# Attention pass of a decoder layer: ScalarE's squares, the energy product and the scale put in another place

## The chip, the cores and the metric

The kernel runs on one core of one Trainium2 chip. The metric is the device time of one execution in microseconds (us); several runs are taken and the median is given.

## What is computed

The layer has a self-attention that reduces to a layer norm of x (a general path for inputs that need it is behind a branch and is not taken here), a cross attention against a context, and a feed-forward part. The change touches the cross attention, for 16 batches of 256 rows by 2048 columns:

```
sim = einsum('ncs,nds->ncd', key, query) * C ** (-0.5)
sim = softmax(sim, axis=1)
context = einsum('ncd,nds->ncs', sim, value)
x = layernorm(x + context)
```

Key and value are both the context input, the query is the normalised x. Products are made of float16 pairs (a high and a low part), so the context is first brought to a power-of-two scale that comes from its sum of squares.

## The kernel before

`attention_pass` (tag "fast") runs the 16 batches as a software pipeline, written out by hand on each engine. `batch_slots` calls `slot(n, ...)` for n = -2 to 15. In slot n each engine works on up to three batches: the end of batch n (its context products, additions and second norm), the middle of batch n + 1 (transposing its normalised x into q, logits, softmax, a guard transform) and the beginning of batch n + 2 (statistics and first norm of x, sum of squares, scale, high and low parts of the values). Tiles that two batches need are doubled and chosen by parity. Each engine runs its instructions in the order written; a wait on a semaphore holds up everything behind it on that engine.

TensorE's slot (`slot` under `block.tensor`): three transposed banks of q (L612), the guard's inverse products (L638), then eight context groups of six products (L625), each of the first five followed by another transposed bank; then the logits of batch n + 1 in two groups of 48 products (L649, `logits(0)` and `logits(1)`), and the guard's forward transform (L689). A transposed bank p waits until bank p - 3 is free, that is until VectorE has made its q_lo. The energy product (L600, `context_energy`) adds the sums of squares of batch n + 2 over the partitions; it stands between the seventh and the eighth context group, and in slot -1 behind the first logits group. `logits(1)` waits for `scale_ready`, because the energy's result lies in its bank.

ScalarE's slot: eight q_hi copies of transposed banks (L347, `emptied_bank`), and between them the deviation squares of the second norm (L391, `spread2`), its application (L397, `normalise2`) and four half-tile squares of the context (L355, `square_context`, 128 x 1024 with an accumulated sum). Then `normalise2` of the first half, the high parts of the values (L422, `value_high`, which waits for the scale), the first norm (L377), exponentials (L384), squares of a weight tile (L370, in slot -1 and odd slots) and of the guard (L428). The squares of the context wait for the context's load, first half in `cbuf0`, second half in `cbuf1`; each also waits for the square before it.

VectorE's slot: eight times q_lo of a bank (L470, `emptied_bank`) and a context addition (L495), with the guard's maxima (L476) between; then `context_scale` (L484, L100 to L102, L486), the mean (L459, L461), statistics of x for batch n + 2 (L552, `x_stats(0)`), low parts of the values (L529), softmax maxima (L536), folds (L565), `x_stats(1)`, probabilities (L543 to L545).

SyncE issues every load and store on one queue, in order: the stores of batch n - 1 (L245, the second waits for `normalise2`), the weight tile in slot -1 and odd slots (L239), the two halves of x for batch n + 2 (L252, each waits until the context additions of batch n are done with its half), the transposes of the keys (L229) and the context for batch n + 3 (L221).

Of the kernel before, what the change touches and what calls it, by code (L numbers as in the profile page):

```python
# [39 lines left out]
KT = L // P  # L40
# [50 lines left out]
def is_batch(n, nb):  # L91

    return not isinstance(n, int) or 0 <= n < nb
# [18 lines left out]
def attention_pass(nc, src, ctx_in, x2_out, w_chunks, b_rows, ag_in, consts, stored, eps_column, tag):  # L112
# [3 lines left out]
    nb = src.shape[0] // C  # L116
    w_rows = w_chunks.rearrange("c p o -> (c p) o")
    PIECES = 2 * R
    with ExitStack() as st:
# [92 lines left out]
        CG = R * NBANK  # L212

        with nc.Block() as block:
# [121 lines left out]
            def _(act):  # L336
                def slot(n, half, parity):
                    cur, nxt, n2 = is_batch(n, nb), is_batch(n + 1, nb), is_batch(n + 2, nb)
# [10 lines left out]
                    def square_context(i):  # L349

                        if n2:
                            r, at = i // 2, i % 2 * HALF
                            act.wait_ge(c_loaded[r], 16 * (n + 3))
                            after(act, sumsq_done, PIECES * (n + 2) + i)
                            nc.scalar.activation(junk[:], cbuf[r][:, at:at + HALF], ACT.Square,  # L355
                                                 accum_out=sumsq[parity][:, i:i + 1]).then_inc(sumsq_done, 1)
# [43 lines left out]
                    for j in range(CG):  # L400
                        emptied_bank(j)
                        if j == 1 and is_batch(n - 1, nb):
                            spread2(n - 1, other, 1)
                        if j == 3 and is_batch(n - 1, nb):
                            normalise2(n - 1, other, 1)
                        if j == 5 and cur:
                            spread2(n, parity, 0)
                        if 1 <= j <= PIECES and n != -1:
                            square_context(j - 1)
                    if n == -1:  # L410
                        for i in range(PIECES):
                            square_context(i)
                    if cur and n < nb - 1:
                        normalise2(n, parity, 0)
                    if n == nb - 1:
# [30 lines left out]
            def _(dve):  # L446
# [5 lines left out]
                def slot(n, half, parity):  # L452
                    cur, nxt, n2 = is_batch(n, nb), is_batch(n + 1, nb), is_batch(n + 2, nb)
# [34 lines left out]
                    for j in range(CG):  # L488
# [22 lines left out]
                        if j == 4 and n == nb - 1:  # L511
                            chain.link(v.tensor_reduce(tmp2[:, 0:1], g_lags[:], AX.X, ALU.max))
                            v.tensor_scalar(verdict[:, 1:2], tmp2[:, 0:1], -GUARD_GAP, None, ALU.is_gt).then_inc(w_summed, 1)
                    if n != -1:
                        context_scale()
                    if cur:

# [47 lines left out]
                            v.tensor_tensor(u_t[:, :, at], q_hi[:, 0:k, at], q_hi[:, k:KT, at], ALU.subtract).then_inc(folded, 1)  # L565

                    x_stats(0)
                    if n == -1:
                        context_scale()
                    value_low(0)  # L570
                    softmax_max(0)
# [16 lines left out]
            def _(pe):  # L588
                def slot(n, half, parity):
# [52 lines left out]
                    def logits(r):  # L642

                        after(pe, exp_done, R * n + r + 1)
                        terms = [(q_hi, 0), (q_hi, 1), (q_lo, 0)]
                        for i in range(3 * KT):
                            qq, part = terms[i % 3]
                            k = i // 3
                            ins = nc.tensor.matmul(ps_s[r][:, 0:C], qq[:, k, r * P:(r + 1) * P], k_both[other][:, k, part, :],  # L649
                                                   start=(i == 0), stop=(i == 3 * KT - 1))  # L650
                        ins.then_inc(sim_done, 1)
# [7 lines left out]
                    for j in range(CG):  # L659
                        if cur:  # L660
                            context(j)
                        if j + 3 < TQ:
                            transposed_bank(j + 3)
                        if j == 6 and n == nb - 1:
                            pe.wait_ge(w_summed, 4)
                            nc.tensor.matmul(verdict_all, ones[:], verdict[:], start=True, stop=True).then_inc(w_reduced, 1)
                        if j == 6 and n != -1:
                            context_energy()
                    if nxt:

                        pe.wait_ge(k_turned, 16 * 2 * R * (n + 2))
                        pe.wait_ge(t_free, TQ * (n + 1) + TQ // R)
                        after(pe, g_free[1], n + 1)
                        logits(0)
                        if n == -1:
                            context_energy()

                        pe.wait_ge(t_free, TQ * (n + 2))
                        if n2:
                            pe.wait_ge(scale_ready, n + 3)  # L680
                        logits(1)

                        pe.wait_ge(folded, R * (n + 2))
                        if isinstance(n, int) and n == -1:
                            pe.wait_ge(tables_loaded, 32)
                        after(pe, ctx_added, CG * (n + 1))
                        for m in range(4):
                            for k in range(HALF // P):
                                ins = nc.tensor.matmul(ps_f[m][:, 0:C], fwd[:, k, m * P:(m + 1) * P], u_t[:, k, :],  # L689
                                                       start=(k == 0), stop=(k == HALF // P - 1))  # L690
                            ins.then_inc(fwd_done, 1)
# [1266 lines left out]
```

## Time and profile before

| | us |
|---|---|
| median of 3 runs | 1969.69 |
| lowest and highest run | 1968.1, 1973.83 |
| profiled execution, its time | 1971.83 |
| its span in the profile | 1970.0 |
| TensorE busy | 1785.7 (91%) |
| VectorE busy | 1363.3 (69%) |
| ScalarE busy | 794.9 (40%) |
| GpSimd busy | 201.2 (10%) |

The span is what the profile's time stamps cover. Shares of busy time are over the whole span; the attention pass is roughly its first 570 us, the feed-forward part the rest, and the two have different limits, so the pass has to be read by itself. In the rows below PE is TensorE, PEld its weight loads, DVE VectorE, ACT ScalarE, POOL GpSimd, SPq SyncE's queue of DMA issues.

### The profile page before, as it was taken

To read this page: it belongs to the slowest core of one execution; us is meant where nothing else is said; L and a number is where in the kernel's file an instruction comes from. 1 tells how busy PE (TensorE), PEld (TensorE's weight loads), DVE (VectorE), ACT (ScalarE), POOL (GpSimd) and SP (SyncE) were. 2 spreads that over 40 slices of the span, in tenths; PEclk is the share of its full clock that TensorE was granted. 3 is DMA by queue.
4 is the path that set the end of the run, shared out by engine and by line. 5 is a ranking of instruction groups with operands and counts; after the bars stand their busy time and mean duration, and the time that the engine had idled before them with its cause. 6 is when DMAs were issued, how large, how long until landed. Compare 5 with 4: busy or idle time off the path is not lost. (4 is left out here: it accounts for less than half of the span.)

```text
span 1970.0 us, 27015 instructions
## 1 busy us (share of the span) xinstructions
PE 1785.7 (91%) x10194; PEld 957.3 (49%) x10210; DVE 1363.3 (69%) x2605; ACT 794.9 (40%) x939; POOL 201.2 (10%) x358
## 2 busy tenths in 40 slices
PE   3989999999853959999999999997899999999997
PEld 2666665757531425444554445443344444444443
DVE  3878887878759856677766677789655555465463
ACT  5788888788745221222222222233221222213111
POOL 1223232323200000000000000000010010010000
PEclk9999999999985989999999999999899999999999
DMA  8899999999848499999999999955999889988982
GB/s 278 194 279 272 283 251 282 267 282 244 234 181 239 121 237 252 264 255 238 252 249 252 251 240 224 232 171 160 275 262 257 274 222 261 265 247 244 255 243 107
DMA packets 565563, 472.70 MB, mean 240 GB/s; under 512 B 498416, under 2 KB 502512, under 8 KB 544624
## 3 DMA queue, kind: packets, MB, share of 16 engines
q1 hardware_dynamic: 565424, 470.87, 87.6%
q8 instruction: 84, 1.38, 0.3%
q14 instruction: 55, 0.45, 0.1%
HBM read 237.51 MB, written 109.58 MB: 176 GB/s over the span
## 5 line engine op out<-in xcount | busy, mean ns | idle before, releaser
L1558 PE MATMUL bank_f<-w_hi_f,a_cols_f 128*128 128x512 f16 x3584 | 1093.4, 382 | 76.9 <-DMA a_cols_f<-rows_f 61.4
L1558 PE MATMUL bank_f<-w_lo_f,a_cols_f 128*128 128x512 f16 x1792 | 685.0, 382 | 0.0
L1558 PEld LDWEIGHTS bank_f<-w_hi_f,a_cols_f 128*128 128x128 f16 x3584 | 352.8, 98 | 508.0 <-issue 45.4
L1148 ACT ACTIVATE rows_f<-xn_f 128x1024 f16<-128x1024 f32 x78 | 82.4, 1056 | 499.5 <-DMA xn_f<-x_scratch 339.8
L1558 PEld LDWEIGHTS bank_f<-w_lo_f,a_cols_f 128*128 128x128 f16 x1792 | 176.4, 98 | 205.0 <-issue 4.8
L1323 DVE SCALAR_TENSOR_TENSOR y_f<-bank_f,w_iscale_f,y_f 128x512 f32<-128x512 f32 x192 | 134.6, 743 | 169.2 <-PE bank_f L1558 168.9
L649 PE MATMUL ps_s_fast<-k_both_fast,q_hi_fast 128*128 128x256 f16 x1024 | 171.0, 275 | 7.4 <-DMA k_both_fast<-v_lo_fast 6.4
L1284 DVE TENSOR_TENSOR rows_f<-xn_f,rows_f 128x1024 f16<-128x1024 f32 x78 | 94.5, 1211 | 97.3 <-ACT rows_f L1148 97.3
L1323 DVE SCALAR_TENSOR_TENSOR y_f<-bank_f,w_iscale,y_f 128x512 f32<-128x512 f32 x192 | 134.9, 745 | 38.2 <-PE bank_f L1558 32.9
L1284 DVE TENSOR_TENSOR rows_f<-sums_f,rows_f 128x1024 f16<-128x1024 f32 x63 | 76.9, 1221 | 114.5 <-ACT rows_f L1148 114.2
L1148 ACT ACTIVATE rows_f<-sums_f 128x1024 f16<-128x1024 f32 x63 | 66.3, 1053 | 198.8 <-DMA a_cols_f<-rows_f 196.3
L649 PE MATMUL ps_s_fast<-k_both_fast,q_lo_fast 128*128 128x256 f16 x512 | 140.6, 275 | 0.0
L495 DVE SCALAR_TENSOR_TENSOR x2buf_fast<-ps_c_fast,iscale_fast,xbuf_fast 128x512 f32<-128x512 f32 x128 | 95.6, 747 | 42.6 <-PE ps_c_fast L625 42.4
L612 PE MATMUL ps_t_fast<-ident,xbuf_fast 128*128 128x128 f32 x512 | 78.0, 288 | 49.4 <-DVE q_lo_fast L470 36.3
L470 DVE TENSOR_TENSOR q_lo_fast<-ps_t_fast,q_hi_fast 128x512 f16<-128x512 f32 x128 | 87.8, 688 | 40.7 <-ACT q_hi_fast L347 40.6
L649 PEld LDWEIGHTS ps_s_fast<-k_both_fast,q_hi_fast 128*128 128x128 f16 x1024 | 100.9, 99 | 23.3 <-DMA k_both_fast<-v_lo_fast 6.8
L625 PE MATMUL ps_c_fast<-v_hi_fast,p_hi_fast 128*128 128x512 f16 x256 | 99.0, 387 | 0.3 <-DVE x2buf_fast L495 0.3
L625 PE MATMUL ps_c_fast<-v_lo_fast,p_hi_fast 128*128 128x512 f16 x256 | 99.0, 387 | 0.0
L625 PE MATMUL ps_c_fast<-v_hi_fast,p_lo_fast 128*128 128x512 f16 x256 | 98.7, 385 | 0.0
L1200 ACT ACTIVATE cbuf<-cbuf,nb_f,rs_f 128x1024 f32<-128x1024 f32 x16 | 19.8, 1239 | 195.2 <-POOL nb_f L1128 195.2
L612 PEld LDWEIGHTS ps_t_fast<-ident,xbuf_fast 128*128 128x128 f32 x512 | 60.0, 146 | 77.6 <-DVE q_lo_fast L470 57.1
L377 ACT ACTIVATE xbuf_fast<-xbuf_fast,nb_fast,rs_fast 128x2048 f32<-128x2048 f32 x32 | 67.1, 2097 | 41.2 <-POOL nb_fast L299 41.2
(210 smaller groups left out, 2310.8 us busy)
## 6 DMA issues: line engine op xcount, KB each, us to landing
xbuf_fast<-x SPq DMA_DIRECT2D x32, 1024.0 KB, 7.3
x_scratch<-x2buf_fast SPq DMA_DIRECT2D x32, 1024.0 KB, 6.4
y_f<-x_scratch SPq DMA_DIRECT2D x32, 1024.0 KB, 7.9
xn_f<-x_scratch SPq DMA_DIRECT2D x62, 512.0 KB, 4.8
kept_scratch<-a_cols_f SPq DMA_DIRECT2D x45, 512.0 KB, 3.4
xn<-x_scratch SPq DMA_DIRECT2D x45, 512.0 KB, 6.9
a_cols_f<-kept_scratch SPq DMA_DIRECT2D x45, 512.0 KB, 8.9
cbuf<-ctx_in SPq DMA_DIRECT2D x16, 1024.0 KB, 5.9
```

The lines of the kernel that those rows point to most:

```text
L377: nc.scalar.activation(xbuf[parity][:, r], xbuf[parity][:, r], ACT.Identity, bias=nb1[:, r:r + 1], scale=rs1[:, r:r + 1]).then_inc(x1_read ...
L470: v.tensor_tensor(q_lo[at], bank, q_hi[at], ALU.subtract).then_inc(t_free, 1)
L495: v.scalar_tensor_tensor(x2buf[parity][:, r, b * BANK:(b + 1) * BANK], ps_c[j % 2][:], iscale[parity][:], xbuf[parity][:, r, b * BANK:(b + ...
L612: ins = nc.tensor.transpose(bank[:, i * P:(i + 1) * P], xbuf[other][:, r, (kk + i) * P:(kk + i + 1) * P], ident[:])
L625: ins = nc.tensor.matmul(ps_c[j % 2][:], pp[:, d, r * P:(r + 1) * P], vv[parity][:, d, b * BANK:(b + 1) * BANK], start=(i == 0), stop=(i = ...
L649: ins = nc.tensor.matmul(ps_s[r][:, 0:C], qq[:, k, r * P:(r + 1) * P], k_both[other][:, k, part, :], start=(i == 0), stop=(i == 3 * KT - 1))
L1148: nc.scalar.activation(rows[g % 2][:, 0], source(i), ACT.Copy).then_inc(a_hi, 1)
L1200: nc.scalar.activation(data[:, 0], data[:, 0], ACT.Identity, bias=nb_[:, 0:1], scale=rs[:, 0:1])
L1284: v.tensor_tensor(rows[g % 2][:, 1], source(i), rows[g % 2][:, 0], ALU.subtract).then_inc(a_lo, 1)
L1323: v.scalar_tensor_tensor(acc, bank[bank_of(s, origin)][:], (w_iscale if sign > 0 else minus_iscale)[s // NP_][:], acc, ALU.mult, ALU.add). ...
L1558: ins = nc.tensor.matmul(bank[i][:], a_cols[:, i, part + kk, :], ww[:, W_SLOT[i], kk, :], start=(kk == 0 and part == 0 and ww is w_hi), st ...
```

## The change

Four things move, all in `attention_pass`. On ScalarE the four context squares go behind the eighth q bank in every slot (as they were in slot -1), the application of the second norm to the second half goes from behind the fourth bank to behind the fifth, and the deviation square of the first half from behind the sixth bank to behind the seventh. On TensorE the energy product goes from between the context groups into the first logits group, ahead of its product 32 of 48. On VectorE `context_scale` goes from ahead of the mean and the first statistics of x to behind them (as it was in slot -1). Slot -2 runs as before, and slots 14 and 15 have no squares, energy or scale. No instruction is added or removed, and no DMA is moved in the queue.

```diff
@@ ScalarE @@
                         emptied_bank(j)
                         if j == 1 and is_batch(n - 1, nb):
                             spread2(n - 1, other, 1)
-                        if j == 3 and is_batch(n - 1, nb):
+                        if j == 4 and is_batch(n - 1, nb):
                             normalise2(n - 1, other, 1)
-                        if j == 5 and cur:
+                        if j == CG - 2 and cur:
                             spread2(n, parity, 0)
-                        if 1 <= j <= PIECES and n != -1:
-                            square_context(j - 1)
-                    if n == -1:
-                        for i in range(PIECES):
-                            square_context(i)
+                    for i in range(PIECES):
+                        square_context(i)
                     if cur and n < nb - 1:
                         normalise2(n, parity, 0)
@@ VectorE @@
-                    if n != -1:
+                    if n == -2:
                         context_scale()
                     if cur:
...
                     x_stats(0)
-                    if n == -1:
+                    if n != -2:
                         context_scale()
                     value_low(0)
@@ TensorE @@
                         for i in range(3 * KT):
+                            if r == 0 and i == 2 * KT:
+                                context_energy()
                             qq, part = terms[i % 3]
...
-                        if j == 6 and n != -1:
-                            context_energy()
+                    if n == -2:
+                        context_energy()
                     if nxt:
...
                         logits(0)
-                        if n == -1:
-                            context_energy()
```

The diff is three lines shorter, so lines behind L413 carry a number lower by three in the changed kernel.

ScalarE before, in slot 1, from the first context square to the last two q banks (junk with sumsq is a context square, junk2 a deviation square, q_hi a bank):

```order
L355 ACTIVATE junk_fast,sumsq1_fast<-cbuf0 128x1024
L347 ACTIVATE q_hi_fast<-ps_t2_fast 128x4x128
L355 ACTIVATE junk_fast,sumsq1_fast<-cbuf0 128x1024
L347 ACTIVATE q_hi_fast<-ps_t0_fast 128x4x128
L397 ACTIVATE x2buf0_fast<-x2buf0_fast,nb2_fast,rs2_fast 128x2048
L355 ACTIVATE junk_fast,sumsq1_fast<-cbuf1_fast 128x1024
L347 ACTIVATE q_hi_fast<-ps_t1_fast 128x4x128
L355 ACTIVATE junk_fast,sumsq1_fast<-cbuf1_fast 128x1024
L347 ACTIVATE q_hi_fast<-ps_t2_fast 128x4x128
L391 ACTIVATE junk2_fast,ssq21_fast<-x2buf1_fast,nmean21_fast 128x2048
L347 ACTIVATE q_hi_fast<-ps_t0_fast 128x4x128
L347 ACTIVATE q_hi_fast<-ps_t1_fast 128x4x128
```

The same slot in the changed kernel, from the third q bank to the first high part of the values:

```order
L347 ACTIVATE q_hi_fast<-ps_t2_fast 128x4x128
L347 ACTIVATE q_hi_fast<-ps_t0_fast 128x4x128
L347 ACTIVATE q_hi_fast<-ps_t1_fast 128x4x128
L397 ACTIVATE x2buf0_fast<-x2buf0_fast,nb2_fast,rs2_fast 128x2048
L347 ACTIVATE q_hi_fast<-ps_t2_fast 128x4x128
L347 ACTIVATE q_hi_fast<-ps_t0_fast 128x4x128
L391 ACTIVATE junk2_fast,ssq21_fast<-x2buf1_fast,nmean21_fast 128x2048
L347 ACTIVATE q_hi_fast<-ps_t1_fast 128x4x128
L355 ACTIVATE junk_fast,sumsq1_fast<-cbuf0 128x1024 x2
L355 ACTIVATE junk_fast,sumsq1_fast<-cbuf1_fast 128x1024 x2
L397 ACTIVATE x2buf1_fast<-x2buf1_fast,nb2_fast,rs2_fast 128x2048
L419 ACTIVATE v_hi1_fast<-cbuf0,scale1_fast 128x2048
```

The four squares have left the banks and stand between the last bank and the norm of the first half (x2buf1), ahead of the high parts.

VectorE before, in slot 1, from the last context addition to the first statistics (L484 to L486 is the scale, BN_STATS the statistics of x):

```order
L495 SCALAR_TENSOR_TENSOR x2buf_fast,x2sum_fast<-ps_c_fast,iscale_fast,xbuf_fast 128x512
L484 TENSOR_REDUCE tmp_fast<-ps_s_fast 128x1
L100 TENSOR_SCALAR tmp_fast<-tmp_fast 128x1
L101 TENSOR_SCALAR scale_fast<-tmp_fast 128x1
L102 TENSOR_SCALAR iscale_fast<-tmp_fast 128x1
L486 TENSOR_SCALAR lscale_fast<-iscale_fast 128x1
L459 TENSOR_REDUCE tmp_fast<-x2sum_fast 128x1
L461 TENSOR_SCALAR nmean_fast<-tmp_fast 128x1
L552 BN_STATS stats_fast<-xbuf_fast 128x6 x4
```

And in the changed kernel:

```order
L492 SCALAR_TENSOR_TENSOR x2buf_fast,x2sum_fast<-ps_c_fast,iscale_fast,xbuf_fast 128x512
L456 TENSOR_REDUCE tmp_fast<-x2sum_fast 128x1
L458 TENSOR_SCALAR nmean_fast<-tmp_fast 128x1
L549 BN_STATS stats_fast<-xbuf_fast 128x6 x4
L74 MEMSET pad 128x1
L554 BN_AGGR mv_fast<-stats_fast 128x2
L481 TENSOR_REDUCE tmp_fast<-ps_s_fast 128x1
L100 TENSOR_SCALAR tmp_fast<-tmp_fast 128x1
L101 TENSOR_SCALAR scale_fast<-tmp_fast 128x1
```

The scale's chain stands behind the mean, the statistics and their aggregate, and so behind the load of x.

## Rows read from the trace of the kernel before

**Rows 1.** Busy time by stretches, all engines: stretch, length, PE, PEld, DVE, ACT, POOL, PEclk, DMA share.

```profile
63.40:527.70 464.30, 428.38 (x3039) 303.84 (x3053) 382.76 (x882) 383.74 (x502) 127.98 (x248) 0.99 0.94 264
```

**Rows 2.** Timeline of TensorE, slots 8 and 9: start, duration, instruction, idle before and releaser.

```profile
343.61 0.38 PE L649 MATMUL ps_s_fast<-k_both_fast,q_hi_fast 128*128 128x256 f16 x2
...
343.94 0.38 PE L649 MATMUL ps_s_fast<-k_both_fast,q_hi_fast 128*128 128x256 f16 x2
...
360.62 0.38 PE L625 MATMUL ps_c_fast<-v_hi_fast,p_hi_fast 128*128 128x512 f16 x1
...
366.13 0.66 PE L612 MATMUL ps_t_fast<-ident,xbuf_fast 128*128 128x128 f32 x4 [0.57 <-DVE q_lo_fast L470]
...
372.00 0.66 PE L612 MATMUL ps_t_fast<-ident,xbuf_fast 128*128 128x128 f32 x4 [2.19 <-DVE q_lo_fast L470]
...
376.51 0.38 PE L649 MATMUL ps_s_fast<-k_both_fast,q_hi_fast 128*128 128x256 f16 x2
```

**Rows 3.** Busy time in the stretch from T of slot 8 to C of slot 9.

```profile
343.60:360.60 17.00, 16.95 (x148) 14.62 (x148) 16.26 (x38) 12.80 (x14) 6.97 (x10) 1.00 0.92 202
```

**Rows 4.** Timeline of ScalarE, slots 8 and 9.

```profile
346.03 2.00 ACT L422 ACTIVATE v_hi_fast<-cbuf,scale_fast 128x2048 f16<-128x2048 f32 x1 [0.39 <-DVE lscale_fast L486]
...
366.19 2.13 ACT L397 ACTIVATE x2buf_fast<-x2buf_fast,nb_fast,rs_fast 128x2048 f32<-128x2048 f32 x1
369.58 1.06 ACT L355 ACTIVATE junk_fast<-cbuf_fast 128x1024 bf16<-128x1024 f32 x1 [1.26 <-DMA cbuf_fast<-ctx_in]
```

**Rows 5.** Timeline of TensorE, slot 14: first context product and first logits product.

```profile
527.71 0.38 PE L625 MATMUL ps_c_fast<-v_hi_fast,p_hi_fast 128*128 128x512 f16 x1
...
541.87 0.38 PE L649 MATMUL ps_s_fast<-k_both_fast,q_hi_fast 128*128 128x256 f16 x2
```

**Rows 6.** Timeline of ScalarE, slot 14: the last two q banks.

```profile
540.39 1.06 ACT L347 ACTIVATE q_hi_fast<-ps_t_fast 128x512 f16<-128x512 f32 x2
```

**Rows 7.** Timeline of ScalarE, slot -1: two squares in a row, and the high values.

```profile
44.27 1.06 ACT L355 ACTIVATE junk_fast<-cbuf_fast 128x1024 bf16<-128x1024 f32 x1 [2.81 <-DMA cbuf_fast<-ctx_in]
...
45.51 1.06 ACT L355 ACTIVATE junk_fast<-cbuf_fast 128x1024 bf16<-128x1024 f32 x1
46.47 0.19 ACT L355 ACTIVATION_READ_ACCUMULATOR junk_fast<-cbuf_fast 128x1 f32 x1
49.72 2.00 ACT L422 ACTIVATE v_hi_fast<-cbuf,scale_fast 128x2048 f16<-128x2048 f32 x1 [3.06 <-DVE lscale_fast L486]
```

**Rows 8.** Timeline of TensorE, slot -1's energy product and slot 0's first context product.

```profile
48.58 0.28 PE L600 MATMUL ps_s_fast<-sumsq_fast,ones_fast 128*128 128x4 f32 x2
...
63.40 0.39 PE L625 MATMUL ps_c_fast<-v_hi_fast,p_hi_fast 128*128 128x512 f16 x1
```

**Rows 9.** Timeline of VectorE, slot -1: the scale's first step and the first low part.

```profile
48.90 0.16 DVE L484 TENSOR_REDUCE tmp_fast<-ps_s_fast 128x1 f32<-128x4 f32 x1 [10.35 <-PE ps_s_fast L600]
...
51.76 2.35 DVE L529 SCALAR_TENSOR_TENSOR v_lo_fast<-cbuf,scale_fast,v_hi_fast 128x2048 f16<-128x2048 f32 x1 [2.07 <-ACT v_hi_fast L422]
```

**Rows 10.** Timeline of SyncE's queue, slot 9: the weight tile and the two x loads.

```profile
368.72 0.46 SPq L239 DMA_DIRECT2D xn<-w_chunks  x1
369.22 9.27 SPq L252 DMA_DIRECT2D xbuf_fast<-x  x2
```

**Rows 11.** Timeline of VectorE, slot 9: the first statistics of x.

```profile
379.94 2.47 DVE L552 BATCH_NORM_STATS2 stats_fast<-xbuf_fast 128x6 f32<-128x512 f32 x4 [0.84 <-DMA xbuf_fast<-x]
```

**Rows 12.** Waits of VectorE from 60 to 545 us: total, times, longest.

```profile
DVE stats_fast L552 <- DMA xbuf_fast<-x: 4.8, 4, 1.7
```

**Rows 13.** One tile's view, x's buffer from 402 to 416 us (slot 10).

```profile
DMA to landing us min/median/max: 6.0/6.9/7.7
```

**Rows 14.** Busy time of the context parts of slots 1, 3 and 11, columns as above.

```profile
94.70:112.40 17.70, 14.82 (x72) 7.51 (x71) 11.97 (x28) 15.68 (x22) 2.22 (x8) 0.90 1.01 338
161.70:177.50 15.80, 13.18 (x72) 7.04 (x71) 11.06 (x26) 14.03 (x22) 2.22 (x8) 1.00 1.06 314
426.50:444.00 17.50, 14.81 (x71) 7.46 (x70) 11.82 (x28) 15.65 (x22) 2.22 (x8) 0.90 0.96 328
```

## The prediction

> **What bounds the kernel now.** I read the busy time by stretches first. The attention pass in its steady state, from the first context product of slot 0 to that of slot 14, takes 464.3 us for 14 slots, 33.2 us each; TensorE is busy for 428.4 us of it, VectorE and ScalarE for about 383 us each, the DMA engines for 0.94 of the time [rows 1]. Three engines and the DMA queue are all close to full, so what matters is the order in which they wait for each other. The change touches this stretch alone (and slot -1 before it), so everything after slot 14 stays as it is.
>
> Then I read one slot on TensorE's timeline, and cut it in two at marks that are easy to find: C, the first context product, and T, the first logits product. In slot 8, T is at 343.61; C of slot 9 is at 360.62, T of slot 9 at 376.51 [rows 2]. So the part behind T (logits, forward transform, three transposes, inverse) takes 17.01 us and the context part 15.89 us. In the first part TensorE has no gap: over 17.00 us TensorE is busy for 16.95 and VectorE for 16.26 [rows 3]. That part is TensorE-bound, with VectorE a hair behind. In the context part TensorE stands twice, 0.57 and 2.19 us, for a q_lo bank [rows 2]. The long one comes from ScalarE: behind a normalisation (366.19) it waits 1.26 us for the context's second half to land before it can square it at 369.58, and the next q bank stands behind that square [rows 4].
>
> **What the change removes.** With all squares behind the eighth bank, no bank waits for a context load. How long is the context part then? Slot 14 shows it, since it has no squares to do: C at 527.71, T at 541.87, 14.2 us [rows 5]. I take 14.2 for every slot. Against slot 9 that is 1.7 us gained; the bound from below is no gain.
>
> **What it adds, on ScalarE.** The squares now start when the last bank is out. In slot 14 the deviation square of the first half is done, and the last two banks start, at 540.39; they take 0.53 us each [rows 6]. The change puts one of the two ahead of the deviation square, so the last bank ends at 540.9, which is T - 1.0. Four squares follow one another. Slot -1 already runs them so: the third starts at 44.27, the fourth at 45.51, and its accumulator is read by 46.66 [rows 7], so 1.24 us from start to start and 1.15 us for the last, 4.87 us together. They end at T + 3.9. Between the banks they were cheaper, but there they stood in the way of the banks. Then the normalisation of the first half, which used to stand right behind the banks, takes some 2.0 us of ScalarE [rows 4], up to T + 5.9.
>
> **What it adds, on TensorE and VectorE.** The energy product stands ahead of product 32 of the 48 of the first logits. Three products take 0.33 us (343.61 to 343.94 [rows 2]), so product 32 is due at T + 3.5 and waits 0.5 us for the squares. In slot -1 the product is at 48.58 [rows 8], VectorE reads it at 48.90 [rows 9] and ScalarE starts the high part of the values at 49.72 [rows 7]: 1.1 us from product to values. Here that gives T + 5.1. VectorE's first statistics, which now stand ahead of the scale, take 2.47 us [rows 11] and some 0.2 us to combine; today the high values start at 346.03 [rows 4], T + 2.4, with 0.8 us of scale work ahead of them, so the last context addition is done by T + 1.6 and the statistics by T + 4.4. They cost nothing if their x is there. So ScalarE, at T + 5.9, is the last, and the high values start 3.5 us later than today.
>
> What hangs on that start is again what slot -1 shows: from the high values (49.72) to the next C (63.40 [rows 8]) it took 13.7 us, a chain in which VectorE waits 2.07 us for the first high half [rows 9] and then works through low values, maxima, folds, second statistics and the probabilities in fixed order. So the part behind T becomes 5.9 + 13.7 = 19.6 us in place of 17.0. The cover of this chain was VectorE's 16 us of work [rows 3], which starts right behind the context part; the change spends that cover by putting the scale late. TensorE's own 17 us are no longer the limit; its 0.5 us at the energy product is hidden.
>
> An even slot is then 14.2 + 19.6 = 33.8 us.
>
> **Odd slots.** These also fetch a weight tile, ahead of x in the same queue. In slot 9 the tile is issued at 368.72 and x at 369.22 [rows 10]; VectorE's statistics start only at 379.94, having waited 0.84 us for that load [rows 11]: x lands at C + 19.3. Such waits came four times, 4.8 us together, 1.7 us the longest [rows 12]. So far only the statistics and the work behind them waited. Now the scale stands behind the statistics, and behind the scale the high values, the second logits group and everything else. x is still issued behind the fourth context addition, which does not move against C; the store and the weight tile ahead of it go out some 1.2 us sooner, because the normalisation they wait for is no longer behind two squares. I take a landing at C + 18.7 (from C + 18.0 to C + 19.3), which is T + 4.5. Statistics of 2.7 us and 0.8 us of scale put the high values at T + 8.0, and the slot is 18.7 + 3.5 + 13.7 = 35.9 us. Ends: 33.8 us where x is no obstacle, 36.5 us where it lands as in slot 9.
>
> **The sum.** 7 x 33.8 + 7 x 35.9 = 487.9 us against 464.3 (slots 0 to 13): +23.6. Slot -1 gains: its product stood behind the first logits at 48.58 though its squares ended at 46.66, so the scale comes at most 1.9 us sooner; I take -1.7. Together **+21.9 us**. The sum is made against the profiled execution, 1971.83 us with a span of 1970.0; the median of the runs is 1969.69, so the forecast is 1969.7 + 21.9 = **1991.6 us**. About 0.3%, 5.9 us, is what a measurement of this kernel can tell from no change.
>
> **A price that is in dispute.** x lands 10.7 us behind its issue in slot 9, but in slot 10, which loads no weights, the two x transfers took 6.0 and 7.7 us [rows 13]. The Trainium skill's page "DMA: Bandwidth & Descriptors", section "Measured (HBM→SBUF, 128 partitions, SWDGE, issued from GpSimd)", gives 6.15 us of DMA time for a 1 MB load, measured there on another queue and alone. By that page's 6.15 us x would be there at C + 14.8, as an estimate, no statistic would wait, and the sum would be about +7; this trace, with the DMA engines 0.94 busy, does not agree for the odd slots. I go by the 10.7.
>
> **The rivals.**
> 1. *x comes in time in odd slots too.* At the 7.7 us of slot 10 it lands at C + 16.3, T + 2.1; the statistics end at T + 4.8 and the scale at T + 5.6, still ahead of ScalarE. Then all 14 slots take 33.8: 473.2 against 464.3, less 1.7, is +7.2, **1976.9 us**. For it: the queue ahead of x is fed earlier. Against it: x is waited for in four slots already, and the statistics that want it will start about 1 us sooner behind T than now. Chance 0.18.
> 2. *Faster: the late scale is hidden.* If the high values started by T + 3.3, the part behind T would stay at TensorE's 17.0 us, and only the shorter context part would be left: 14 x 31.2 = 436.8, less 464.3 and 1.7, is -29, **1940.5 us**. It decides at the end of the squares: they would have to end by T + 1.3, and their start at T - 1.0 and 4.87 us speak against it. A half-way case (squares shorter by 1 us and x in time) still gives about no change. Chance of faster 0.07; of no change, 0.11.
> 3. *The clock.* In slot 1, with a granted clock of 0.90 over its context part (the half level, 1.2 GHz, for a fifth of it), that part took 17.7 us; slot 3 at 1.00 took 15.8 [rows 14]. Three slots are of that kind, the last of them slot 11, with 17.5 us at 0.90. If the new stalls, in odd slots 2 us in front of the second logits and in all slots about 1 us at the transform, bring this to the context part of all seven odd slots, it costs up to 7 x 2 us more: **2005.6 us**. Against it: a lower clock behind T is covered by the 19.6 us chain. Chance 0.12.
> 4. *The change does nothing.* The instruction order shows each of the three moves in every slot from 0 to 13, so this has no chance of its own.
>
> **How the numbers follow.** Forecast 0.52, rival 1 0.18, rival 3 0.12, no change 0.11, faster 0.07. The forecast's own range, from the ends of the x landing and 0.5 us in the chain per slot, is 1983 to 2000. To hold 8 in 10 the range takes in rival 1 and most of rival 3: **1974 to 2006**. Rival 1 lies just over the 0.3% line, so a sliver of it counts as no change: slower 0.80, same 0.13, faster 0.07.
>
> **What would show it.** Right: context parts of about 14.2 us with no stall over 1 us; 19 to 20 us from T to C in even slots; high values at about T + 6 in even and T + 8 in odd slots; VectorE waiting for x in most odd slots, with TensorE standing in front of the second logits there. ScalarE's wait for the context load is gone. Wrong: if the part behind T stays near 17 us, the chain from the squares is not what ends last; if VectorE never waits for x, the odd slots are priced too high; if context parts stay near 15.8, the banks were held by something else.

## The result: 33.5 us slower

The changed kernel takes 2003.89 us (median; 2001.56 to 2005.80) beside 1970.34 us (1968.10 to 1973.83) for the kernel before: a ratio of 1.0161, 95% interval 1.0148 to 1.0175. The sign and the mechanism are those of the prediction. The time lies inside its range of 1974 to 2006 us, but above the forecast's own range of 1983 to 2000; the forecast of 1991.6 us is 12.3 us short. The profiled execution of the changed kernel took 2001.56 us with a span of 1999.8 us.

I read it as the kernel before was read: busy time by stretches first (stretch, length, PE, PEld, DVE, ACT, POOL, PEclk, DMA share, GB/s). The rows are the steady state from C of slot 0 to C of slot 14, then slot 4's context part, slot 4's part behind T, and slot 1's part behind T.

```profile
61.40:559.50 498.10, 438.24 (x3039) 301.67 (x3052) 384.17 (x882) 388.06 (x502) 98.03 (x248) 0.98 0.86 246
204.07:218.23 14.16, 13.00 (x70) 6.71 (x70) 11.57 (x28) 11.04 (x15) 2.19 (x8) 1.00 0.97 310
218.23:237.74 19.51, 17.76 (x150) 14.57 (x150) 15.86 (x36) 15.97 (x22) 4.89 (x11) 1.00 0.84 189
109.09:133.51 24.42, 19.91 (x150) 15.82 (x150) 15.96 (x36) 18.34 (x26) 4.90 (x11) 0.86 0.82 209
```

The 14 slots take 498.1 us in place of 464.3 [rows 1], with the same work: VectorE is busy for 384 us in place of 383, ScalarE for 388 in place of 384, TensorE for 438 in place of 428 (at a granted clock of 0.98 in place of 0.99). The engines stand more, and the DMA share falls from 0.94 to 0.86. The context part is 14.15 to 14.17 us in every slot from 0 to 14. All the loss lies behind T: over the 14 slots the context parts take 198.2 us in place of 219.9, the parts behind T 300.0 in place of 244.4. It is of two sizes.

**Even slots.** TensorE's timeline of slot 4 (start, duration, instruction, idle before and releaser): C, T, the energy product, the forward transform, and C of slot 5.

```profile
204.07 0.39 PE L622 MATMUL ps_c_fast<-v_hi_fast,p_hi_fast 128*128 128x512 f16 x1
...
218.23 0.38 PE L648 MATMUL ps_s_fast<-k_both_fast,q_hi_fast 128*128 128x256 f16 x2
...
222.14 0.38 PE L597 MATMUL ps_s_fast<-sumsq_fast,ones_fast 128*128 128x4 f32 x2 [0.26 <-ACT junk_fast L355]
...
230.29 2.79 PE L686 MATMUL ps_t_fast<-ag_raw,fwd_fast 128*128 128x256 bf16 x24 [0.76 <-DVE ag_raw L562]
...
237.74 0.39 PE L622 MATMUL ps_c_fast<-v_hi_fast,p_hi_fast 128*128 128x512 f16 x1
```

ScalarE's timeline of the same slot: the first and the last of the four squares, the norm of the first half, the first high values.

```profile
217.23 1.04 ACT L355 ACTIVATE junk_fast<-cbuf 128x1024 bf16<-128x1024 f32 x1
...
220.94 1.06 ACT L355 ACTIVATE junk_fast<-cbuf_fast 128x1024 bf16<-128x1024 f32 x1
221.99 2.08 ACT L397 ACTIVATE x2buf_fast<-x2buf_fast,nb_fast,rs_fast 128x2048 f32<-128x2048 f32 x1
224.07 2.00 ACT L419 ACTIVATE v_hi_fast<-cbuf,scale_fast 128x2048 f16<-128x2048 f32 x1
```

The squares end at T + 3.8 (with the last accumulator read, T + 3.9) and the norm holds ScalarE to T + 5.8, where the high values start; C follows 13.7 us later. (In this slot the scale is ready within 0.1 us of that; in slots 0, 2, 6 and 10, where x came earlier, the high values start at T + 5.75.) VectorE's timeline of slot 4 shows what that costs: the statistics start once x has landed, the scale's first step follows them, and the first low part waits 2.13 us for the high values.

```profile
220.55 2.47 DVE L549 BATCH_NORM_STATS2 stats_fast<-xbuf_fast 128x6 f32<-128x512 f32 x4 [0.98 <-DMA xbuf_fast<-x]
...
223.24 0.10 DVE L481 TENSOR_REDUCE tmp_fast<-ps_s_fast 128x1 f32<-128x4 f32 x1
...
226.10 2.35 DVE L526 SCALAR_TENSOR_TENSOR v_lo_fast<-cbuf,scale_fast,v_hi_fast 128x2048 f16<-128x2048 f32 x1 [2.13 <-ACT v_hi_fast L419]
```

In the kernel before the high values started at T + 2.4 [rows 4], and the same part took 17.0 us [rows 3].

**Odd slots.** VectorE's timeline of slot 5 (T at 251.90): the mean, the statistics, the last step of the scale, the first low part.

```profile
253.08 0.15 DVE L458 TENSOR_SCALAR nmean_fast<-tmp_fast 128x1 f32<-128x1 f32 x1
257.88 2.47 DVE L549 BATCH_NORM_STATS2 stats_fast<-xbuf_fast 128x6 f32<-128x512 f32 x4 [4.64 <-DMA xbuf_fast<-x]
...
261.15 0.15 DVE L483 TENSOR_SCALAR lscale_fast<-iscale_fast 128x1 f32<-128x1 f32 x1
263.43 2.35 DVE L526 SCALAR_TENSOR_TENSOR v_lo_fast<-cbuf,scale_fast,v_hi_fast 128x2048 f16<-128x2048 f32 x1 [2.13 <-ACT v_hi_fast L419]
```

VectorE stands 4.64 us for x where slot 9 before stood 0.84 [rows 11] and no slot more than 1.7 [rows 12], and now the scale stands behind it. ScalarE's timeline of slot 5 has the wait that follows, and TensorE's has the next: the second logits group.

```profile
255.67 2.08 ACT L397 ACTIVATE x2buf_fast<-x2buf_fast,nb_fast,rs_fast 128x2048 f32<-128x2048 f32 x1
261.39 2.00 ACT L419 ACTIVATE v_hi_fast<-cbuf,scale_fast 128x2048 f16<-128x2048 f32 x1 [3.65 <-DVE lscale_fast L483]
```

```profile
257.69 0.27 PE L648 MATMUL ps_s_fast<-k_both_fast,q_lo_fast 128*128 128x256 f16 x1
261.40 0.58 PE L648 MATMUL ps_s_fast<-k_both_fast,q_hi_fast 128*128 128x256 f16 x2 [3.44 <-issue]
```

The view of the waits from 60 to 560 us adds them up (total, times, longest): VectorE, ScalarE, TensorE.

```profile
DVE stats_fast L549 <- DMA xbuf_fast<-x: 38.5, 13, 5.4
...
ACT v_hi_fast L419 <- DVE lscale_fast L483: 26.6, 9, 4.4
...
PE ps_s_fast L648 <- issue: 24.7, 9, 4.2
PE ps_t_fast L609 <- DVE q_lo_fast L467: 16.2, 28, 0.6
```

VectorE waits for x 38.5 us in place of 4.8 [rows 12]. The nine slots in which ScalarE waits for the scale are the seven odd ones and slots 8 and 12. TensorE's longest wait for a q_lo bank has fallen from 2.3 us to 0.6 (16.2 us in all in place of 32.2), and ScalarE no longer waits for the context load: that is the part of the change that works. The same view of the kernel before had

```profile
PE ps_t_fast L612 <- DVE q_lo_fast L470: 32.2, 30, 2.3
...
ACT junk_fast L355 <- DMA cbuf_fast<-ctx_in: 13.0, 11, 2.9
```

Slot by slot the timelines give: even slots 0, 2, 4, 6 and 10 take 33.6 to 33.7 us, slots 8 and 12 take 34.9 and 34.8; the odd slots take 36.2 to 38.6, mean 37.2. C of slot 0 comes at 61.36 us, 2.04 sooner than before.

### The profile page after: what moved, and what is told of

Read it like the earlier page. It is cut to its first block, busy times and chain, and to the rows that moved or that the text cites. A ratio compares the mean times of both kernels' runs of the same rounds, so it can differ in the third digit from the quotient of the medians.

```text
span 1999.8 us, 27015 instructions
## 1 busy us (share of the span) xinstructions
PE 1794.6 (90%) x10194; PEld 955.0 (48%) x10210; DVE 1364.2 (68%) x2605; ACT 799.5 (40%) x939; POOL 171.1 (9%) x358
## 4 chain that ended last, share of the span: by engine, by line
PE 51%; DVE 8%; DMA 6%; issue 3%; SPq 1%; ACT 1%; ACTq 0%; POOL 0%; DVEq 0%; POOLq 0%
PE bank_f L1555 46%; DMA a_cols_f<-rows_f 5%; DVE w_lo_f L1289 2%; DVE y_f L1320 1%; PE bank_f L1574 1%; PE bank_f L1593 1%; PE bank_f L1594 1%; DVE rows_f L1281 1%; SPq L949 1%; ACT rows_f L1145 1%; PE bank_f L1575 1%; DMA xn_f<-x_scratch 0%; DMA y_f<-w_chunks 0%; DVE xn L1294 0%; DVE sums_f L1274 0%
## 5 line engine op out<-in xcount | busy, mean ns | idle before, releaser
L648 PE MATMUL ps_s_fast<-k_both_fast,q_hi_fast 128*128 128x256 f16 x1024 | 179.2, 281 | 31.2 <-issue 24.7
L492 DVE SCALAR_TENSOR_TENSOR x2buf_fast<-ps_c_fast,iscale_fast,xbuf_fast 128x512 f32<-128x512 f32 x128 | 95.8, 748 | 35.4 <-PE ps_c_fast L622 35.3
L609 PE MATMUL ps_t_fast<-ident,xbuf_fast 128*128 128x128 f32 x512 | 79.4, 287 | 37.7 <-DVE q_lo_fast L467 20.9
L549 DVE BATCH_NORM_STATS2 stats_fast<-xbuf_fast 128x6 f32<-128x512 f32 x128 | 79.0, 679 | 38.5 <-DMA xbuf_fast<-x 38.5
```

The lines of the kernel that those rows point to most:

```text
L492: v.scalar_tensor_tensor(x2buf[parity][:, r, b * BANK:(b + 1) * BANK], ps_c[j % 2][:], iscale[parity][:], xbuf[parity][:, r, b * BANK:(b + ...
L549: ins = v.bn_stats(stats[:, r, b], xbuf[parity][:, r, b * BANK:(b + 1) * BANK])
L609: ins = nc.tensor.transpose(bank[:, i * P:(i + 1) * P], xbuf[other][:, r, (kk + i) * P:(kk + i + 1) * P], ident[:])
```

## The experiments

**Theory M** (two chains): the high values wait for the later of two chains, squares, norm (T + 5.75) and x's load, statistics, scale (landing + 3.5 us), and C follows 13.7 us behind them. **Theory R1**: the squares behind the banks are the whole cost. **Theory R2**: the scale behind the statistics is the whole cost. The first four kernels each change one thing of the changed kernel. Their common median for the kernel before is 1971.29 us.

**1. The scale ahead of the statistics again.**

```diff
@@ changed kernel, VectorE @@
-                    if n == -2:
-                        context_scale()
+                    context_scale()
...
                     x_stats(0)
-                    if n != -2:
-                        context_scale()
```

> The changed kernel with VectorE's part undone: the scale stands ahead of the mean and the first statistics of x again. Theory M (two chains ahead of the high values: squares, norm, high values, ready at T + 5.75; and in odd slots x load, statistics, scale, at T + 8.4 to 10.3): the second chain is cut, high values at T + 5.75 in all slots, some odd slots still 1 to 1.7 us longer because the statistics now delay the low values; 14 slots take about 476 us in place of 498, about 1981 us. Rival R1 (the squares behind the banks are the whole cost): nothing changes, 2004 us. Rival R2 (the scale behind the statistics is the whole cost): 17.0 us behind T again with the short context part, about 1949 us.

Measured: 1988.01 us (1986.25 to 1991.81), ratio to before 1.0089 (1.0068 to 1.0109). The view of VectorE's waits:

```profile
DVE tmp_fast L481 <- PE ps_s_fast L594: 47.3, 14, 3.4
...
DVE stats_fast L548 <- DMA xbuf_fast<-x: 2.6, 3, 1.4
```

VectorE now waits for the energy product, 3.4 us in every slot, and for x in three slots only. High values start at T + 5.75 in all 14 slots, the odd ones too; the part behind T takes 19.55 us in even and 20.07 to 21.8 in odd slots. Some 16 us are gone and some 17 remain, against both R1 (2004) and R2 (1949). The time is 7 us above M's 1981: the 14 slots take 479.0 us where M had 476, since every odd slot is 0.5 us or more longer than the even ones, and by the profiles C of slot 0 comes 1.3 us later and the stretch behind slot 14, which the edit does not touch, is 2.6 us longer.

**2. ScalarE's order of before, the rest as changed.** The energy product and the scale stay late.

```diff
@@ changed kernel, ScalarE @@
-                        if j == 4 and is_batch(n - 1, nb):
+                        if j == 3 and is_batch(n - 1, nb):
                             normalise2(n - 1, other, 1)
-                        if j == CG - 2 and cur:
+                        if j == 5 and cur:
                             spread2(n, parity, 0)
-                    for i in range(PIECES):
-                        square_context(i)
+                        if 1 <= j <= PIECES and n != -1:
+                            square_context(j - 1)
+                    if n == -1:
+                        for i in range(PIECES):
+                            square_context(i)
```

> The changed kernel with ScalarE's part undone: squares between the banks, norm and deviation square where they were. M: the context part is 15 to 16 us again (sometimes 17.5 with a lower clock), the scale still waits for the statistics and x, high values at T + 5.3 in even and T + 7.5 in odd slots, so nothing is won: about 2008 us (2000 to 2013). R1: the loss goes away, 1970 us or less. R2: as M, the loss stays.

Measured: 2012.09 us (2010.66 to 2013.24), 1.0202 (1.0184 to 1.0220). The view of TensorE's waits has the old wait back, longer than it was:

```profile
PE ps_t_fast L612 <- DVE q_lo_fast L470: 41.0, 28, 3.1
```

Context parts take 14.9 to 18.8 us again, six of them 17 or more. So R1 falls: with no square moved the kernel is slower still. Given the late scale, moving the squares is worth about 8 us by the medians; of the profiled executions the 14 slots alone differ by 5.5 us.

**3. The weight tile behind the first half of x.** In the changed kernel's SyncE queue the tile stood ahead of x.

```diff
@@ changed kernel, SyncE @@
                             sp.dma_start(xbuf[parity][:, r], src[bass.ds(n * C + r * P, P), :]).then_inc(x_loaded[parity][r], 16)
+                            if r == 0 and n > 1:
+                                load_weights(n)
...
                         store(n - 1, 1 - parity)
-                        load_weights(n + 2)
                         if n > -1:
                             load_x(n + 2, parity)
+                        else:
+                            load_weights(n + 2)
```

> The changed kernel with the weight tile issued behind the first half of x instead of ahead of both. M: x lands in odd slots as in even ones, T + 1.3 to 3.5, the high values start at T + 5.8 to 7, odd slots take 33.6 to 35 us in place of 36 to 38.6: about 1981 us. R1: nothing changes, 2004 us. If the DMA engines' total load and not the order in the queue makes x late, little changes either, 1998 to 2004 us.

Measured: 1986.96 us (1986.08 to 1988.77), 1.0076 (1.0058 to 1.0093). The view of VectorE's waits:

```profile
DVE stats_fast L552 <- DMA xbuf_fast<-x: 22.9, 13, 3.1
```

The statistics of odd slots start at T + 3.0 to T + 4.5 (mean 3.5) where they started at T + 4.9 to T + 6.7 (mean 5.8), though x is issued at the same time. One transfer's place in the queue carries half of the loss. The time is 6 us above M's 1981: x still came later than in M's even slots (T + 4.5 in slot 9), so odd slots take 34.4 to 35.8 us where M had 33.6 to 35.

**4. Two of the squares early**, in the steps j == 5 and j == 6 of the banks, the other two behind all banks.

```diff
@@ changed kernel, ScalarE @@
+                        for i in {5: (0,), 6: (1,)}.get(j, ()) if cur else ():
+                            square_context(i)
...
-                    for i in range(PIECES):
+                    for i in (2, 3) if cur else range(PIECES):
                         square_context(i)
```

> The changed kernel with the two squares of the context's first half in the time in which ScalarE stands idle, one behind the sixth and one behind the seventh bank; the other two stay behind the eighth. The squares end at T + 1.4 in place of T + 3.9. M: the scale still waits for x and the statistics, in even slots until T + 4.8 to 5.75, so only up to 0.9 us in a few even slots and nothing in odd ones: about 2001 us (1998 to 2004). R1: 2.4 us less in each of 14 slots, about 1970 us.

Measured: 2002.99 us (2000.53 to 2007.89), 1.0163 (1.0138 to 1.0187), the changed kernel's time. The view of the waits, VectorE and ScalarE:

```profile
DVE stats_fast L551 <- DMA xbuf_fast<-x: 39.1, 13, 5.2
...
ACT v_hi_fast L421 <- DVE lscale_fast L485: 60.0, 14, 6.7
```

Context parts stay at 14.16, the squares end at T + 1.4, and ScalarE spends what it gained waiting for the scale, in all 14 slots now. As M has it, shortening the chain of the squares alone buys nothing while x's chain ends last. (Even slots, in which the two chains end close together, gain 2.7 us in all; odd slots, in which x landed a little later still, lose 3.7.)

**5. The edits of kernels 1 and 3 together**, on the changed kernel, with the squares left behind all banks. If the two gains of 16 us were independent, the loss would be gone.

> The changed kernel with both of the edits that alone took 16 us off it: the scale ahead of the first statistics, and the weight tile behind the first half of x. The squares stay behind all banks. If the two gains are independent they add, 2004 - 16 - 16 = 1972 us. Theory M (two chains, the later of which starts the high values): both edits take away the same chain, that of x, and the chain of the squares stays: context part 14.16, high values at T + 5.75 and 19.5 from T to C in every slot, odd ones too, so 14 x 33.7 = 472 in place of 498, and about 1978 us, some 7 above the kernel before. In that case the chain of the squares alone is worth +7 and that of x +26 on top.

Measured: 1980.96 us (1980.39 to 1982.59) beside 1971.64, 1.0046 (1.0029 to 1.0063). VectorE's waits, and busy time behind T of slots 2 and 3:

```profile
DVE tmp_fast L484 <- PE ps_s_fast L597: 47.3, 14, 3.4
```

```profile
145.28:164.82 19.54, 17.81 (x152) 14.54 (x150) 15.67 (x36) 15.75 (x22) 7.01 (x11) 1.00 0.77 195
178.98:199.06 20.08, 18.02 (x151) 14.62 (x150) 15.67 (x36) 17.82 (x26) 7.02 (x11) 1.00 0.92 267
```

No wait for x is left, and high values start at T + 5.75 in every slot. The gains don't add: both edits shorten the same chain, that of x, and the chain of the squares keeps 9 us. That is a net price: against the kernel before the parts behind T are 33.2 us longer over the 14 slots, the context parts 21.7 us shorter. The median is 3 us above what M gave: odd slots are 0.5 us longer than M had, since there ScalarE squares the weight tile, and the second exponential comes at T + 16.9 in slot 3 and at T + 16.3 in slot 2.

**6. Both chains shortened:** the edits of kernels 1 and 3, three squares among the last banks, and the energy product ahead of product 6 in place of 32.

```diff
@@ kernels 1 and 3 and, on ScalarE and TensorE @@
+                        for i in {5: (0,), 6: (1, 2)}.get(j, ()) if cur else ():
+                            square_context(i)
...
-                    for i in range(PIECES):
+                    for i in (3,) if cur else range(PIECES):
                         square_context(i)
...
-                            if r == 0 and i == 2 * KT:
+                            if r == 0 and i == 6:
                                 context_energy()
```

> The changed kernel with both chains cut at once: one square behind the sixth bank, two behind the seventh, one behind the eighth (they end at about T + 0.3); energy product ahead of product 6 of the first logits (due at T + 0.7); scale ahead of mean and statistics; weight tile behind the first half of x. M: context part 14.2 us, high values at T + 2.4 as in the kernel before, 17.0 us behind T, 31.2 us per slot plus up to 1 us in slots in which x still lands late, 437 to 450 us for 14 slots against 464: about 1955 us (1944 to 1962). If the DMA engines (busy for 0.94 of the time in the kernel before) now set the pace, slots stay above 32.5 us: 1962 to 1970.

Measured: 1950.71 us (1948.98 to 1952.71), **0.9893 (0.9878 to 0.9908)** of the kernel before (1972.44 us beside this and the next three): faster than both. Busy time of its steady state and behind T of slot 6:

```profile
65.80:508.59 442.79, 423.87 (x3040) 300.63 (x3052) 382.39 (x882) 382.64 (x502) 127.92 (x248) 1.00 1.01 275
269.63:286.78 17.15, 17.10 (x150) 14.76 (x150) 15.67 (x36) 13.05 (x17) 7.04 (x11) 1.00 0.98 228
```

Context parts are 14.15 us, high values start at T + 2.1 in all slots but two, and behind T TensorE is busy for 17.10 of 17.15 us. Against the kernel before the 14 slots take 21.5 us less, and all of it lies in the context parts (198.2 us in place of 219.9); the parts behind T are as long as they were (244.6 and 244.4). The DMA share is now 1.01 over the whole stretch, and in some slots the statistics wait for x again, until T + 4.56 at the latest. I take the transfers to be the next limit; no run tests that.

**7. The same with two squares early** ({5: (0,), 6: (1,)}, two behind the banks) and the energy product ahead of product 16.

> As the one before, with two squares early and two behind the eighth bank (end T + 1.4) and the energy product ahead of product 16 (due at T + 1.8). M: scale at T + 2.9, high values at T + 3.4, statistics until T + 5.6, so 17.2 to 17.4 us behind T, 31.5 us per slot: about 1958 us, up to 1% under the kernel before. If squares ahead of the last bank delay that bank, the context part is over 14.5 us and the gain is smaller.

Measured: 1954.25 us (1953.06 to 1956.86), 0.9911 (0.9898 to 0.9925). High values start at T + 3.27: 1.2 us later than in kernel 6, for 3.5 us in all. Up to there TensorE's own 17 us nearly cover the chain, which is the point the second rival of the prediction gave (T + 3.3).

**8. The kernel before with the tile behind the first half of x only** (the edit of kernel 3).

> The kernel before with only the weight tile issued behind the first half of x. M: the waits for x in slots 3, 5, 9 and 13 (1.2 to 2.0 us longer there) go away and nothing else changes: about 6 us less, 1965 us. If x is late because of the DMA engines' total load, no change, 1971 us.

Measured: 1969.22 us (1965.41 to 1973.23), 0.9984 (0.9973 to 0.9995), half of what was expected. VectorE's waits, and the busy time of the context parts of slots 1 and 7:

```profile
DVE stats_fast L555 <- DMA xbuf_fast<-x: 0.3, 1, 0.3
```

```profile
93.50:111.04 17.54, 14.80 (x71) 7.54 (x70) 11.86 (x28) 15.65 (x22) 2.23 (x8) 0.90 1.03 342
292.41:306.93 14.52, 13.13 (x71) 7.01 (x70) 11.03 (x26) 13.87 (x22) 2.23 (x8) 1.00 0.97 333
```

The wait for x is gone and the part behind T is 17.01 to 17.28 us in all slots, 4.9 us less over the 14 slots. But context parts go on varying, from 14.3 to 19.2 us, and are 3.2 us longer in all. So in the old order, with the squares among the banks, most of what there is to win is lost there (why these parts came out longer is not shown); in the new order the same edit is worth 17 us.

**9. ScalarE's part of the change alone.** Scale ahead of the statistics, and the energy product between the last context product and the first logits.

```diff
@@ changed kernel, TensorE (and the scale as in kernel 1) @@
-                            if r == 0 and i == 2 * KT:
-                                context_energy()
...
-                    if n == -2:
-                        context_energy()
+                    context_energy()
                     if nxt:
```

> The kernel before with ScalarE's part alone: squares behind the banks, scale ahead of mean and statistics as before, energy product between the last context product and the first logits, the nearest place at which it does not hold up the context part. M: TensorE stands at T until the squares end at T + 3.9, then needs its 17.0 us: 21 us behind T, 35.2 us per slot, about 2000 us, up to 10 us more if the stall lowers the clock. It shows what moving the energy product into the logits saves. R1 in another form (late squares cost by ScalarE's chain alone): as the run with the scale ahead and the product inside the logits, 1988 us.

Measured: 2027.34 us (2024.20 to 2030.41), 1.0277 (1.0260 to 1.0293), 17 us above the far end of the expectation. TensorE's timeline in front of slot 1's logits, and busy time behind T of slots 1 and 7:

```profile
120.08 0.38 PE L594 MATMUL ps_s_fast<-sumsq_fast,ones_fast 128*128 128x4 f32 x2 [3.75 <-ACT junk_fast L355]
```

```profile
120.33:139.00 18.67, 18.62 (x149) 15.47 (x150) 14.90 (x33) 14.72 (x19) 6.83 (x10) 0.91 0.82 171
344.99:362.00 17.01, 16.96 (x150) 14.61 (x151) 14.72 (x33) 14.55 (x19) 6.99 (x10) 1.00 0.89 185
```

TensorE stands 3.75 us for the squares, as expected (C to T is 18.3 to 18.5 us). What was not expected stands in the second fence: in or behind that stall the granted clock fell in 13 of 14 slots, and the same work took 18.7 to 19.5 us; in slot 7, after the same stall, it stayed at 1.00 and the part took 17.01. With no slack behind T the lower clock is paid in full: the parts behind T are 25 us longer over the 14 slots than at 17.01 each, which is nearly all that the expected 2000 us lacked.

## Why the prediction was right, and where it was short

**The context part** (14.2 us in every slot) was right: 14.15 to 14.17. **Slot -1** (-1.7 us) was right: -2.04.

**The chain from the squares** (19.6 us behind T, high values at T + 5.9) was right: T + 5.75 and 19.4 to 19.5 us in the five even slots in which x was in time. Kernel 5, where this chain stands alone, shows it in every slot, and prices it at 9 us net of the shorter context parts.

**The term that was too small is x's landing in odd slots.** I took C + 18.7, that is T + 4.5, and an odd slot of 35.9 us. It landed at T + 4.85 to T + 6.74, mean 5.80, that is C + 20.0, beyond the later end of my bounds (C + 19.3). From the landing on, the terms hold: 3.52 us to the high values, and 13.7 us from there to C in six of the seven slots, 14.2 in slot 1. The odd slots so take 9.2 us more than forecast, nearly all of it this one term (7 x 1.3); slots 8 and 12, where x was late too (statistics at T + 3.5), add 2.1, and the other even slots give 1 back. Together 10.3 us: 498.2 where 487.9 was forecast. (With slot -1 the profiled executions differ by 31.8 us up to C of slot 14, and behind it the changed kernel's is 2.0 us shorter, where the change touches nothing; the medians differ by 33.5.)

The later end of my bounds was itself too early. I read it off slot 9, but the kernel before had waited longer in other odd slots, in slot 5 (C at 227.48) until C + 19.95:

```profile
247.43 2.47 DVE L552 BATCH_NORM_STATS2 stats_fast<-xbuf_fast 128x6 f32<-128x512 f32 x4 [1.68 <-DMA xbuf_fast<-x]
```

By the landing itself, some 0.03 us ahead of the statistics, x came at C + 18.8 to C + 19.9 in its seven odd slots, mean 19.3; in the changed kernel it is C + 19.0 to C + 20.9, mean 19.9. So about half of the 1.3 us is the earlier landing that did not come, and the other half is that x landed 0.6 us later than before.

The reason I gave for an earlier landing was that the store and the weight tile go out some 1.2 us sooner. They do. SyncE's queue in slot 5 (C at 237.74):

```profile
236.72 3.41 SPq L229 DMA_TRANSPOSE k_both_fast<-v_lo_fast  x1
240.18 0.58 SPq L221 DMA_DIRECT2D cbuf_fast<-ctx_in  x1
240.80 3.78 SPq L245 DMA_DIRECT2D x_scratch<-x2buf_fast  x2
244.62 0.66 SPq L239 DMA_DIRECT2D xn<-w_chunks  x1
246.04 7.18 SPq L252 DMA_DIRECT2D xbuf_fast<-x  x2
```

The tile goes out at C + 6.9 in place of C + 8.1 and x at C + 8.3 in place of C + 8.6 [rows 10]. But the DMA view of 222 to 262 us, in 40 slices of 1 us, shows what decides:

```profile
DMA  9300069990999959999949999999999999993000
GB/s 410 164 0 0 0 134 213 201 121 10 290 283 226 179 172 385 387 182 240 231 66 336 246 344 410 426 459 426 401 410 451 401 401 410 442 401 164 41 0 0
```

From 246 us, when x is issued, to 258, when it has landed, every slice carries 401 to 459 GB/s. Some 420 GB/s over 11.8 us are 5 MB, about x and the four 1 MB transfers issued last ahead of it (context half, two stores, tile). I read this so: in such a queue x lands when the bytes ahead of it have gone, and an issue 0.3 us sooner moves nothing. One place further forward should then be worth 1 MB at 420 GB/s, 2.5 us; kernel 3 moved x by one place, and it came 2.3 us sooner. What made it 0.6 us later than before is only argued: the head of the queue hangs on the delayed values. In the odd slots the context's second half is issued at C + 1.4 to C + 2.1 before (mean 1.8) and at C + 1.7 to C + 3.2 now (mean 2.3), behind key transposes that wait for the low values; on the mean that gives 0.5 of the 0.6 us, though not slot by slot (in slot 1 it is issued as before and x lands 1.6 us later).

Kernel 9 fits this reading. There the high values start 15 to 18 us ahead of the next C in place of 13.7 to 14.2, and SyncE's queue in slot 5 (C at 251.76) has

```profile
250.31 1.21 SPq L221 DMA_DIRECT2D cbuf_fast<-ctx_in  x1
...
260.05 0.33 SPq L252 DMA_DIRECT2D xbuf_fast<-x  x1
```

The context half goes out at C - 1.5 to C + 0.4 in odd slots; x, issued at C + 8.3 behind the same transfers as in the changed kernel, lands at C + 16.2 to C + 17.3. It is no clean test, since the odd slots of kernel 9 are 35.3 to 38.0 us long for other reasons. Why slots 8 and 12 were late and the other even ones not stays open; in the kernel before, too, they were the even slots in which x landed last (C + 16.9 and 16.8, the others 13.2 to 16.1).

**The price in dispute.** The 6.15 us for a 1 MB load that the Trainium skill's page "DMA: Bandwidth & Descriptors" gives in its section "Measured (HBM→SBUF, 128 partitions, SWDGE, issued from GpSimd)" is far from the odd slots here. The page says that its figures are of a single core with the pair's other core idle; it does not say what else was in flight. The tile's view of x's buffer from 236 to 262 us has

```profile
DMA to landing us min/median/max: 7.4/9.6/11.8
```

**The rivals.** Rival 1 (x in time in odd slots) fell: VectorE waited in 13 slots. Its price of 33.8 us a slot, 1976.9 us in all, is nearly kernel 5's 1981. Rival 2 (the late scale is hidden) fell where the prediction put it, at the end of the squares (T + 3.8, not T + 1.3), and kernels 6 and 7 show the other side of it. Rival 3 (the clock in the context parts) did not come: the granted clock fell behind T of slots 1 (0.86 over the part), 5, 7 and 9, and in no context part; the chain on VectorE covered it but for some 0.5 us in slot 1. It was partly luck that the time lies inside the stated range: the range reached beyond 2000 us for the sake of this rival, and what used that room was x's landing.

## What to carry to other kernels

When a step is put behind a load that was off the path, price the load anew: by the bytes that stand ahead of it in a full queue, not by its own issue time; then try another place in the queue, which cost nothing here and gave 17 us in the changed kernel, 3 us in the kernel before. When two chains end at one wait, shortening the one that ends first gives next to nothing (kernel 4), and two edits that shorten the same chain do not add: 16 and 17 us alone, 23 together. A move that loses may be right in half: the squares out of the way of the banks are worth having once the scale comes early, the tile stands behind x, and a few squares fill ScalarE's idle time between the last banks.

## What was not expected of the hardware

A stall of 3.75 us on TensorE in front of the logits cost a further 1.7 us or more in 13 of 14 slots of kernel 9, because the granted clock then fell (0.91 over the 18.67 us behind it, 1.00 in slot 7). In the changed kernel, after stalls of up to 4.2 us in front of the second logits, the pairs of products behind the stall in slot 5 took 0.63 us in place of 0.38 for a while, and the slot lost nothing by it, since VectorE's chain was longer. A stall's price thus depends on what stands behind it.
